# One-hots of the second segment-sum pass: from one VectorE compare to nine ScalarE activations

## The reference: what is computed

```python
def sage_conv(x, edge_index, W_l, b_l, W_r, num_segments):
    src, dst = (edge_index[0], edge_index[1])
    agg = jax.ops.segment_sum(x[src], dst, num_segments=num_segments)
    return agg @ W_l.T + b_l + x @ W_r.T
...
h = jax.nn.relu(sage_conv(x, edge_index, W_l_in, b_l_in, W_r_in, n))
out = sage_conv(h, edge_index, W_l_out, b_l_out, W_r_out, n)
```

## Time and profile before

| | us |
|---|---|
| median of 3 runs | 4493.09 (4488.0 to 4493.76) |
| the profiled execution | 4485.84 |
| its span | 4484.0 |
| second pass, read phase and first ten units | 1242.8 to 1813.4 |
| second pass, rest of the unit phase | 1813.4 to 2050.4 |

### The profile page before, as it was taken

One profiled execution on the slowest core, in us unless ns is written; L12 is line 12 of the kernel. 1 busy time (PEld: TensorE's weight loads), 2 busy tenths in 40 slices (PEclk: granted clock), 3 DMA queues, 4 the chain that ended last, 5 costly groups with the idle time before them and its releaser, 6 DMA issues. The chain is left out here.

```text
span 4484.0 us, 83127 instructions
## 1 busy us (share of the span) xinstructions
PE 3313.8 (74%) x27012; PEld 2537.2 (57%) x27012; DVE 2665.5 (59%) x7125; ACT 2007.6 (45%) x5442; POOL 3192.6 (71%) x3086
## 2 busy tenths in 40 slices
PE   3879999999878778997455666666767767666556
PEld 2545555555556666556444565665656656656456
DVE  8847766665122222566223668768678687686776
ACT  2667878777200000784000454655546546555310
POOL 4756777776477777773777777777777777777473
PEclk9999999999588999999555677777667676677666
DMA  2434556555199999002334554555545545555331
GB/s 85 188 128 188 219 222 240 218 222 191 38 360 379 367 363 359 14 14 74 88 86 93 133 132 124 140 134 130 136 119 150 132 121 147 129 136 132 87 99 48
DMA packets 353117, 713.23 MB, mean 159 GB/s; under 512 B 127521, under 2 KB 211419, under 8 KB 344640
## 3 DMA queue, kind: packets, MB, share of 16 engines
q1 hardware_dynamic: 258848, 634.44, 40.2%
q0 software_dynamic: 92160, 74.67, 10.5%
q10 hardware_dynamic: 1800, 0.10, 0.0%
HBM read 446.37 MB, written 262.54 MB: 158 GB/s over the span
## 5 line engine op out<-in xcount | busy, mean ns | idle before, releaser
L1662 POOL DMA_INDIRECT gath<-fs_scratch,src_idx x1568 | 1588.4, 1013 | 486.2 <-issue 472.3
L1768 ACT ACTIVATE scratch<-scratch,bias,weight 128x32 f32<-128x32 f32 x2608 | 932.5, 400 | 776.4 <-DVE bias L1843 776.4
L674 POOL DMA_INDIRECT gath<-in_x,src_idx x720 | 760.5, 1056 | 319.3 <-issue 269.4
L722 ACT ACTIVATE scratch<-sum_x_ps_c 128x800 bf16<-128x800 f32 x932 | 754.8, 837 | 248.7 <-PE sum_x_ps_c L741 240.0
L674 POOL DMA_INDIRECT gath<-y_scratch,src_idx x592 | 607.2, 1026 | 191.5 <-issue 178.9
L1698 PE MATMUL ps_e<-gath,ident 128*128 128x264 f32 x784 | 339.2, 574 | 539.4 <-DMA gath<-fs_scratch,src_idx 539.2
L1718 PE MATMUL ps_m<-scratch 128*64 128x128 f32 x3136 | 575.1, 360 | 70.4 <-POOL scratch L1685 65.7
L1704 PEld LDWEIGHTS ps_e<-fdw,scratch 128*128 128x128 f32 x3136 | 572.4, 273 | 57.1 <-issue 24.1
L1718 PEld LDWEIGHTS ps_m<-scratch 128*64 128x64 f32 x3136 | 516.7, 189 | 97.7 <-issue 41.4
L1704 PE MATMUL ps_e<-fdw,scratch 128*128 128x66 f32 x3136 | 555.2, 354 | 22.3 <-DMA fdw<-fd_scratch 22.3
L1854 DVE SCALAR_TENSOR_TENSOR scratch<-ps_e,attn_sb 128x128 f32<-128x128 f32 x784 | 190.2, 285 | 608.0 <-PE ps_e L1704 606.7
(11 more groups left out here) (274 smaller groups left out, 4141.0 us busy)
## 6 DMA issues: line engine op xcount, KB each, us to landing
count_scratch<-scratch SPq DMA_DIRECT2D x60, 3200.0 KB
scratch<-count_scratch SPq DMA_DIRECT2D x240, 800.0 KB
en_scratch<-gath SPq DMA_DIRECT2D x196, 264.0 KB
scratch<-en_scratch SPq DMA_DIRECT2D x196, 264.0 KB
onehot<-rel_scratch SPq DMA_DIRECT2D x198, 256.0 KB
scratch<-in_edge_attr_2x SPq DMA_DIRECT2D x390, 128.0 KB
gath<-fs_scratch,src_idx POOLq DMA_INDIRECT x1568
fdw<-fd_scratch SPq DMA_DIRECT2D x392, 33.0 KB
```

What stands on the lines that cost most here:

```text
L674: pool.indirect_dma_start(out=gath[:, s, t, 0:F], out_offset=None, in_=table_dram, in_offset=bass.IndirectOffsetOnAxis(ap=src_idx[:, g, k: ...
L722: act.activation(counts[:, b % 2, :, unit["column"]:unit["column"] + 2 * q] .rearrange("p a (h d) -> p h a d", h=2), ps_c[u % 3][:, :, 0:q ...
L1662: pool.indirect_dma_start(out=gath[:, s, t, :], out_offset=None, in_=fs_dram, in_offset=bass.IndirectOffsetOnAxis(ap=src_idx[:, g, k:k + 1 ...
L1768: e = act.activation(rows, rows, ACT.Exp, bias=bias[:, q, i:i + 1], scale=weight[:, q, i:i + 1], accum_out=total[:, q, i:i + 1] if i < K * ...
```

## The change

In the second pass (`read` is 60 there, 0 in the first pass) the one-hots are made by ScalarE in place of VectorE. For each of the 8 tiles an activation takes the square of `dst_rel - iota`; a wait on the new semaphore `distant` follows; then one activation over all 8 tiles takes `relu(1 - 2 d^2)`, which is 1 where the distance is 0 and 0 where it is 1 or more. ScalarE's program becomes a walk over the steps: in a step the unit's copy first (`keep`), then, where a slot begins, the next slot's one-hot. VectorE writes a column of ones once, in the set-up, and keeps the one-hots of the first pass.

```diff
+        unit_col = sb("unit_col", [P, 1])
...
+                dve.memset(unit_col[:, :], 1.0)
...
                 @block.scalar
                 def _(act):
-                    if values is not None:
-                        act.activation(parts[:, :, 0:F], values, ACT.Copy).then_inc(cut, 1)
-                    for u, unit in enumerate(head.units[plan.first_unit:plan.end_unit]):
+                    def keep(u):
+                        unit = head.units[plan.first_unit + u]
...
+                    def make_onehot(i):
+
+                        if i >= 2:
+                            act.wait_ge(summed, i - 1)
+                        for t in range(ST):
+                            g, k = (n0 + i) * SG + t // K, t % K
+                            far = act.activation(onehot[:, i % 2, t, :], iota[:, :], ACT.Square,
+                                                 bias=dst_rel[:, g, k:k + 1], scale=-1.0)
+                        far.then_inc(distant, 1)
+                        act.wait_ge(distant, i + 1)
+                        act.activation(onehot[:, i % 2, :, :], onehot[:, i % 2, :, :], ACT.Relu,
+                                       bias=unit_col[:, 0:1], scale=-2.0).then_inc(onehot_ready, 1)
+
+                    if values is not None:
+                        act.activation(parts[:, :, 0:F], values, ACT.Copy).then_inc(cut, 1)
+                    if read:
+                        make_onehot(0)
+                    for step in range(plan.steps):
+                        if step in plan.unit_at:
+                            keep(plan.unit_at[step] - plan.first_unit)
+                        for i, t in taken.get(step, ()):
+                            if read and t == 0 and i + 1 < slots:
+                                make_onehot(i + 1)
...
-                    make_onehot(0)
+                    if not read:
+                        make_onehot(0)
...
-                            if t == 0 and i + 1 < slots:
+                            if not read and t == 0 and i + 1 < slots:
                                 make_onehot(i + 1)
```

More of the change, by code:

```diff
@@ L656, in segment_sum_pass @@
                 opened, padded, cells_made, counted, kept, cut, less, multiplied, summed_up, windowed, \
-                    head_added, onehot_ready, summed, tail_added, turned, placed, quarter_used = map(sem, (
+                    head_added, onehot_ready, summed, tail_added, turned, placed, quarter_used, distant = map(sem, (
                         "opened", "padded", "cells_made", "counted", "kept", "cut", "less", "multiplied",
                         "summed_up", "windowed", "head_added", "onehot_ready", "summed", "tail_added", "turned", "placed",
-                        "quarter_used"))
+                        "quarter_used", "distant"))
                 stored = [sem(f"stored{w}") for w in range(2)]
```

## The result

| | before | after |
|---|---|---|
| median, us | 4493.43 (4488.0 to 4496.29, 4 runs) | 4528.12 (4516.12 to 4531.39, 4 runs) |
| the profiled execution, us | 4485.84 | 4516.12 |
| its span, us | 4484.0 | 4514.3 |

The changed kernel is slower: ratio 1.0074, 95% interval 1.0053 to 1.0094. The forecast, 4517 us, is 11 us short. Only ordinary executions are compared in this document: one of the ten of the last experiment's kernel took 10276.96 us and is left out of its ratio. The two parts of the second pass went opposite ways, as forecast, but the second part lost more.

A forecast was written before the change was run, and what follows sets the result against it. GpSimd's gather issuing was taken to bound the read phase, TensorE the unit phase. Terms: -23 + 39 + 7 - 2 + 3 = +24 us, 4510 on the profiled execution, 4517 us on the median; range 4496 to 4550.

The forecast's parts named there:

- The read phase: Second pass up to slot 53: without VectorE's compare GpSimd issues gathers faster; 23 us gain, bounds 15 to 26.
- The group: ScalarE's eight squares and one relu for a slot's one-hot take 3.6 us together, bounds 2.6 to 5.1.
- The stall: Unit phase, after slot 53: TensorE waits 1.95 us for ScalarE's copy behind each of twenty groups, +39 us.
- s+4: Product of the fourth unit after unit s, behind which a group stands; TensorE was to stall there 1.95 us.
- Block ends: Unit phase: a block's products wait for its last copy; half of 15 ends by 1 us more, +7 us.
- VectorE's relief: Unit phase: 20 compares of 1.23 us leave VectorE, which feeds TensorE's compares; 2 us gain.
- The clock: Unit phase: TensorE idling 2 us in every 13 may lower its granted clock; 0.95 costs 10 us, 3 taken.
- case (D): The forecast itself: a group of 3.3 to 4.0 us, read-phase gain 15 to 26 us, 4505 to 4530; chance 0.52.
- case (C): Unit phase: group up to 5.1 us, or stalls cost the clock its full speed; +60 us, 4553; chance 0.14.
- (A): Unit-phase loss hidden or repaid, kernel faster by over 0.2%: group below 2.3 us or TensorE gains elsewhere; chance 0.06.
- (B): Read-phase gain doesn't come: counts hold it, compare isn't the delay, or ScalarE delays issues likewise; +47 us, 4540; chance 0.18.
- the page's inference: Skill page on SBUF: VectorE's two-SBUF-input compare leaves descriptor generation alone, so wouldn't delay gathers; read-phase gain would be nothing.

The follow-up runs named there:

- the last experiment's kernel: Changed kernel, unit phase in thirds: VectorE's compare; ScalarE's group plus extra TensorE products; ScalarE's activations behind nine copies. 4485.94 us against 4491.07 before, ratio 0.9988.
- The third with filled stalls: Units 92 to 174 of the last experiment's kernel: ScalarE's group as changed, plus five unread TensorE products before the wait at s+4; 94.7 us against 99.3.
- the variants: Four kernels: ScalarE's one-hots to slot 52 only, from slot 54 only, in nine pieces, or with TensorE's stalls filled; ratios 1.0099, 1.007, 1.0149, 1.017.

## Why the prediction was right, step by step

**The read phase (-23 us; measured -24.8).** The chain was the gathers' issuing, and it was the compare that stretched it; both are shown by the compare with an operand in PSUM. The counts stayed second at 377 GB/s (the forecast wanted over 375), though they took more of TensorE's time than before. By the forecast's own figures they were 25 us ahead of the gathers (1785.5 - 1760), not 20.

**The group (3.6 us; measured 3.6).** Squares take 386 ns each at the median and 2.44 us for eight that follow one another, the relu 1.15 us. ScalarE's groups in the read phase don't delay gathers: of 159 issues that began inside one of its squares or relus, 4 were long, by 0.25 us together. The Trainium skill (ScalarE: Activation LUTs, "What ACT_TABLE_LOAD costs") would have given the alone-standing ones as 387 and 1133 ns by its formula; the trace's 386 and 1148 agree.

**The stall (39 us; measured 33.8).** It stands at s+4, and its size is right: the 17 full stalls are 1.94 us on average, against 1.95. Their number is not: of twenty groups, one had a stall of only 0.6 us, and two stalled TensorE at a block's end.

**Block ends (7 us; measured 8.8), VectorE's relief (2 us; measured 2.0).** The 7 us were right by luck. They were meant as 1 us more at half of the ends; 6.2 us are the stalls of those two groups, and all the other ends together lost 2.6.

**The clock (3 us; measured 18.8) is the term that was mis-sized.** I weighed a granted 0.95 at 10 us against nothing and took the lower half. I had set the phase beside stretches of a similar average busy share, and the average says nothing on how the idle time lies. Here it lies in 2 us pieces, and beside ten of the 19 long waits the clock fell, so that a pair of products took 0.83 us for 0.51. Which of them it would be, no row of the kernel before could tell. The third with filled stalls shows the cause. The sum by the trace: -24.8 + 33.8 + 8.8 - 2.0 + 18.8 = +34.6 us against +24. The clock's 15.8 us too few and the block ends' 1.8, less the 5.2 us of stalls and the 1.8 us of greater gain, are the 11 us between 4517 and 4528. So the other misses cancelled in part, and the time fell inside case (D), near its upper bound, though case (C) had the clock.

**The rivals.** (A) fell with the group at 3.6 us. (B), with the page's inference, fell with the issues at 0.955 us. (C) was half right: not the group, but the clock; its +8 us for it was also too little.

## What to carry to other kernels

Before an engine is relieved of an instruction, find out what about that instruction hurts: here it was two SBUF inputs beside indirect DMA issues, and the cure that beats both kernels keeps the instruction on VectorE and puts one input in PSUM (4464.91 us, 21 us under the kernel before). Cutting it into eight short ones gives most of the same (4471.05 us), because each holds an issue only to its own end. An experiment that doubles a dose has to be checked for whether the second half can act: here the pace of the issues carried them past the second compare. An engine that feeds another through few buffers has to be costed by its longest burst against those buffers, not by its average. Where TensorE will idle for 2 us at regular places, add to the waits the dearer products behind some of them: here 18.8 us of busy time beside 33.8 us of stalls. Not all of it comes back with the clock: in the third with filled stalls 7.4 us less busy time gave 4.6 us.

## What the runs showed of the hardware

- A VectorE compare of 128x1024 in f32 with both inputs in SBUF holds back an indirect DMA issue of GpSimd that begins inside it, until 0.82 us after its end; with one input in PSUM it doesn't (1.4 us of long issues in 54 slots against 25.2, and 0.76 of the 1.4 stand at the one compare that was left in SBUF).
- An issue that begins in the first 0.03 us of such a compare, or in its last 0.13 us, takes its usual 0.95 us. With two compares in a row every held issue put the next one into the last 0.13 us of the second: 23.3 us of long issues, as with one.
- A 128x128 compare with a scalar per partition holds issues in the same way, to 0.82 us after its own end. It takes 0.28 us, and eight per slot leave 3.9 us of long issues in 54 slots.
- ScalarE's squares and relu with the same two sources in SBUF, one as its bias, hold nothing back: 0.4 us of long issues in 54 slots.
- With TensorE idle for about 1.9 us in some 15, the granted clock fell to its lower level beside 10 of 19 such waits, for 3 to 7 us; with products of 1.3 us at that place the third's granted clock was 0.98 in place of 0.91.
- Two chips ran all of this a quarter slower (5588 and 5582 us against 4486), with TensorE standing in unexplained gaps, and the order of the variants' read phases was another there.
